# Inputs laid out in order of need on one DMA queue, three warm-up products instead of four, and the head's steps put in another order

## What is computed

```python
x = x + L0: x @ (sum_g y[b,g] * weight[g] * mask).T + bias          # a weight per batch
x = x + L1: x @ W_base.T + b_base + 2 * sum_e w[b,e] * (x @ A[e].T) @ B[e].T   # rank 16 each
x = x + L2: sum over the top 2 of 8 experts of w * mlp_e(x) + mlp_shared(x)    # gelu(x@G)*(x@U)@D, 512 wide
x = x + L3: mlp of the argmax expert, silu(up)*gate, 256 wide, with biases
```

## Time and profile before

| | us |
|---|---|
| median of 3 runs | 142.79 (141.63 to 143.33) |
| the profiled execution | 141.64, span 139.8 |
| PE busy | 134.5 (96%) |
| DVE busy | 100.2 (72%) |
| ACT busy | 97.9 (70%) |
| POOL busy | 73.9 (53%) |
| chain that ended last | PE 93% of the span |

### The profile page before, as it was taken

The page is one execution under the profiler, slowest core; times in us unless marked ns, Lnnn a source line. Parts: engine busy times, 40 slices in busy tenths (PEclk is TensorE's granted clock), DMA queues, the critical chain, the costliest instruction groups (busy, mean ns, idle before and its releaser), DMA issues.

```text
span 139.8 us, 3283 instructions
## 1 busy us (share of the span) xinstructions
PE 134.5 (96%) x932; PEld 124.2 (89%) x932; DVE 100.2 (72%) x192; ACT 97.9 (70%) x201; POOL 73.9 (53%) x87
## 2 busy tenths in 40 slices
PE   6989999989999999999999999999999999999991
PEld 5768888768888899999999999999999999999991
DVE  0587898695775957758768577676767766878983
ACT  3394697867985487777877777757657569887770
POOL 0229349772995028358496574962542625325370
PEclk9999999999999999999999999999999999999999
DMA  4899999998000895656756567555576465773215
GB/s 126 261 408 412 403 400 401 400 388 326 9 0 0 334 369 210 259 217 273 291 209 254 210 246 300 224 231 233 217 301 259 199 264 217 279 298 152 77 42 187
DMA packets 11346, 34.56 MB, mean 247 GB/s; under 512 B 1088, under 2 KB 2240, under 8 KB 11328
## 3 DMA queue, kind: packets, MB, share of 16 engines
q1 hardware_dynamic: 11040, 33.82, 61.8%
q10 hardware_dynamic: 288, 0.52, 1.1%
HBM read 12.32 MB, written 1.05 MB: 96 GB/s over the span
## 4 chain that ended last, share of the span: by engine, by line
PE 93%; DVE 2%; ACT 1%; issue 1%; ACTq 0%; DVEq 0%
PE acc L284 31%; PE up L284 31%; PE gate L284 30%; DVE x_res L935 1%; ACT h_hi L589 1%; DVE h_lo L970 0%; ACT out_part L630 0%; ACT h_act L651 0%; DVE slabs L822 0%; ACTq L213 0%; DVE slabs L782 0%; ACTq L607 0%; DVE shift_pick L783 0%; ACT dn_hi L607 0%; ACT h_act L583 0%
## 5 line engine op out<-in xcount | busy, mean ns | idle before, releaser
L721 POOL TENSOR_TENSOR dn_lo<-slabs,dn_hi 128x256 fp32r<-128x256 f32 x40 | 29.6, 739 | 42.7 <-ACT dn_hi L607 42.6
L583 ACT ACTIVATE h_act<-gate 128x512 f32<-128x512 f32 x48 | 28.8, 599 | 27.7 <-PE gate L284 26.3
L875 DVE SCALAR_TENSOR_TENSOR up<-h_act,w_route,up 128x512 f32<-128x512 f32 x32 | 24.2, 756 | 20.5 <-PE up L284 20.5
L865 DVE TENSOR_TENSOR h_lo<-up,h_hi 128x512 fp32r<-128x512 f32 x55 | 37.6, 684 | 0.4 <-ACT h_hi L589 0.4
L284 PE MATMUL gate<-x_hi,w_gu 128*128 128x256 f32 x160 | 35.5, 282 | 0.2 <-ACT h_act L651 0.2
L284 PE MATMUL up<-x_hi,w_gu 128*128 128x256 f32 x160 | 35.4, 281 | 0.0
L589 ACT ACTIVATE h_hi<-up 128x512 fp32r<-128x512 f32 x55 | 32.8, 596 | 0.0
L284 PEld LDWEIGHTS gate<-x_hi,w_gu 128*128 128x128 f32 x160 | 27.6, 189 | 0.7 <-issue 0.4
L284 PEld LDWEIGHTS up<-x_hi,w_gu 128*128 128x128 f32 x160 | 27.7, 189 | 0.0
L284 PE MATMUL up<-x_lo,w_gu 128*128 128x256 f32 x80 | 22.6, 283 | 0.0
L284 PE MATMUL gate<-x_lo,w_gu 128*128 128x256 f32 x80 | 22.6, 283 | 0.0
(11 more groups left out here) (115 smaller groups left out, 213.9 us busy)
## 6 DMA issues: line engine op xcount, KB each, us to landing
w_gu<-slabs SPq DMA_DIRECT2D x40, 512.0 KB, 3.0
slabs<-slabs_moe SPq DMA_DIRECT2D x8, 768.0 KB, 14.8
slabs<-slabs_l SPq DMA_DIRECT2D x4, 768.0 KB, 8.2
outT<-x_res SPq DMA_DIRECT2D x8, 128.0 KB, 2.0
sh_raw<-slabs_shared SPq DMA_DIRECT2D x2, 384.0 KB, 7.5
x_res<-xT SPq DMA_DIRECT2D x1, 768.0 KB, 8.1
slabs<-w_l SPq DMA_DIRECT2D x2, 256.0 KB, 4.1
slabs<-lin ACTq DMA_DIRECT2D x1, 384.0 KB, 4.9
```

The source lines that it names most:

```text
L583: nc.scalar.activation(h_act[:, u % 2, :], gate_ps[u % 2][:], ACT.Gelu_apprx_tanh).then_inc(act_done, 1)
L721: nc.gpsimd.tensor_tensor(dn_lo[:, q % W_SLOTS, :], slab_cols(at, DOWN_AT, 256), dn_hi[:, q % W_SLOTS, :].bitcast(F32), ALU.subtract).then ...
L865: V.tensor_tensor(h_lo[:, u % H_SLOTS, :], h_of(u), h_hi[:, u % H_SLOTS, :].bitcast(F32), ALU.subtract).then_inc(h_lo_done, 1)
L875: ins = V.scalar_tensor_tensor(h_of(u), h_act[:, k, :], weight, h_of(u), ALU.mult, ALU.mult)
```

## The change

Five tensors take the place of four. first_in holds cond and the first half of w_l0 (762 columns), second_in the other half, lora_bT and mask (768 columns), third_in lora_a, w_baseT, ident and lora_aT (512 columns). x is given as two tensors, x_first and x_rest, and the shared weights as two halves, each contiguous in memory. All are issued by SP, in that order; ACT issues none. Warm-up products go from four to three. ACT scales lora_bT for all eight batches, in the order 0 1, 2 3 4 5, 6 7, and DVE for none. ACT rounds the first half of the shared weights ahead of exp_pick and the gelu table. POOL makes the remainder of that half ahead of the slab table. keep_x2 of pairs 2 and 3 stands ahead of product and lo_h.

```diff
-WARM_UP = 4
+WARM_UP = 3
...
-            sp.dma_start(w_l0_sb[:, 0:4, :], w_l0[:, 0:4, :]).then_inc(d_w_l0, DMA)
-            sp.dma_start(w_l0_sb[:, 4:8, :], w_l0[:, 4:8, :]).then_inc(d_w_l0b, DMA)
-            sp.dma_start(x_res[:, 0:PAIR], xT[:, 0:PAIR]).then_inc(d_x, DMA)
-            sp.dma_start(sh_raw[:, 0:SLAB], slabs_shared[:, 0:SLAB]).then_inc(d_shared[0], DMA)
-            sp.dma_start(x_res[:, PAIR:], xT[:, PAIR:]).then_inc(d_x_rest, DMA)
-            sp.dma_start(sh_raw[:, SLAB:], slabs_shared[:, SLAB:]).then_inc(d_shared[1], DMA)
+            sp.dma_start(cond_all[:, :], first_in).then_inc(d_first, DMA)
+            sp.dma_start(second_sb[:, :, :], second_in).then_inc(d_second, DMA)
+            sp.dma_start(third_sb[:, :, :], third_in).then_inc(d_third, DMA)
+            sp.dma_start(x_res[:, 0:PAIR], x_first).then_inc(d_x, DMA)
+            sp.dma_start(sh_raw[:, 0:SLAB], slabs_shared[0]).then_inc(d_shared[0], DMA)
+            sp.dma_start(sh_raw[:, SLAB:], slabs_shared[1]).then_inc(d_shared[1], DMA)
+            sp.dma_start(x_res[:, PAIR:], x_rest).then_inc(d_x_rest, DMA)
...
-            pe.wait_ge(d_lin, DMA)
-            for out, first_b, n, ready in ((gate_ps[0][:, 0:S], 0, 2, bw_first), (up_ps[1][:, 0:S], 6, 2, bw_last),
-                                           (gate_ps[1][:], 2, 4, bw_middle)):
-                pe.wait_ge(ready, 1)
...
+            pe.wait_ge(d_third, DMA)
...
+            pe.wait_ge(bw_ready, 1)
+            lora(gate_ps[0][:, 0:S], 0, 2)
+            mm(acc_ps[:, 512:512 + B], lora_aT, bias_l0.to_broadcast([P, B]), True, True).then_inc(a_bias_sum, 1)
+            pe.wait_ge(bw_ready, 2)
+            lora(gate_ps[1][:], 2, 4)
...
             matrix(0)
+            pe.wait_ge(bw_ready, 3)
+            lora(up_ps[1][:, 0:S], 6, 2)
...
-            act.dma_start(cond_all[:, :], cond).then_inc(d_cond, DMA)
-            act.dma_start(lin_sb[:, :, :], lin).then_inc(d_lin, DMA)
...
-            act.wait_ge(d_lin, DMA)
+            act.wait_ge(d_second, DMA)
             act.wait_ge(scaled_ready, 1)
-            for group, ready in (((6, 7), bw_last), ((2, 3, 4, 5), bw_middle)):
+            for group in ((0, 1), (2, 3, 4, 5), (6, 7)):
...
+            round_shared(0)
             act.wait_ge(top2_ready, 1)
             act.wait_ge(zeros_ready, 2)
             nc.scalar.activation(exp_pick[:], shift_pick[:], ACT.Exp).then_inc(second_ready, 1)
             nc.scalar.activation(table_first[:, 0:1], cond_sb[:, 0, 0:1], ACT.Gelu_apprx_tanh)
...
-            round_shared(0)
...
             nc.gpsimd.tensor_tensor(key[:], hit[:, 1], rows(rank_e, B), ALU.mult).then_inc(key_ready, 1)
+            lo_shared(0)
...
-            lo_shared(0)
             lo_shared(1)
...
-            V.tensor_tensor(lora_bw[:, 0:2], rows(lora_bT, 2),
-                            cond_scaled[:, 0:2].unsqueeze(2).to_broadcast([P, 2, P]),
-                            ALU.mult).then_inc(bw_first, 1)
...
+            mask_w0(0)
             dve.wait_ge(shift_ready, 1)
...
+            mask_w0(1)
             dve.wait_ge(base_ready, 1)
...
-            add_base(1, 6, 2, up_ps[1][:, 0:S])
+            add_base(1, 2, 4, gate_ps[1][:])
+            dve.wait_ge(r1_ready, 1)
+            combine(0)
+            add_base(2, 6, 2, up_ps[1][:, 0:S])
             dve.wait_ge(key_ready, 1)
             V.tensor_reduce(first[:, 1], key[:], AX_X, ALU.max).then_inc(first_ready, 1)
-            dve.wait_ge(r1_ready, 1)
-            combine(0)
             dve.wait_ge(c_sum, 1)
             V.tensor_scalar(c_b[:], acc_ps[:, 0:B], bias_l1, None, ALU.add).then_inc(acc_read, ACC_BIAS)
-            add_base(2, 2, 4, gate_ps[1][:])
...
                 if u - 1 in X2_AFTER_UNIT:
                     split_x2(X2_AFTER_UNIT[u - 1])
+                    if u > 1:
+                        keep_x2(X2_AFTER_UNIT[u - 1])
                 product(u)
                 lo_h(u - 1)
-                if u - 1 in X2_AFTER_UNIT:
-                    keep_x2(X2_AFTER_UNIT[u - 1])
+                if u == 1:
+                    keep_x2(X2_AFTER_UNIT[0])
```

More of the change, by code:

```diff
@@ L65, with build @@
 C_VECS = C_RANK + E
-C_COLS = C_VECS + 2 + 5 * E
-def build(nc, xT, cond, w_l0, lin, slabs_moe, slabs_l3, slabs_shared, outT):
+C_W = C_VECS + 2 + 5 * E
+C_COLS = C_W + 4 * P
+def build(nc, x_first, first_in, second_in, third_in, x_rest, slabs_moe, slabs_l3, slabs_shared, outT):
     with ExitStack() as ctx:
@@ L173, in build @@
         scaled_ready, bias_prod_ready = sem("scaled_ready"), sem("bias_prod_ready")
[L174 to L175 removed]
+        bw_ready, base_ready = sem("bw_ready"), sem("base_ready")
         pool_step = sem("pool_step")
@@ L573, in _ @@
             round_shared(0)
+            act.wait_ge(top2_ready, 1)
+            act.wait_ge(zeros_ready, 2)
+            nc.scalar.activation(exp_pick[:], shift_pick[:], ACT.Exp).then_inc(second_ready, 1)
+            nc.scalar.activation(table_first[:, 0:1], cond_sb[:, 0, 0:1], ACT.Gelu_apprx_tanh)
             act.wait_ge(x2_first_sum, 1)
@@ L973, in _, with cond_layout @@
                 finish(t)
-def cond_layout(cond, vecs):
+def cond_layout(cond, vecs, w_l0):
     p = np.arange(P)
@@ L985, in cond_layout @@
     c[:, C_RANK:C_VECS] = E - np.arange(E)
-    c[:, C_VECS:] = vecs
+    c[:, C_VECS:C_W] = vecs
+    c[:, C_W:] = w_l0.reshape(P, 4 * P)
     return c
```

63 lines of the change are left out of this document (28 added, 35 removed).

## The result

| | median of the runs | ratio to before (95% interval) | profiled execution |
|---|---|---|---|
| before | 141.94 us (22 runs) | | 141.64, span 139.8 |
| changed | 141.38 us (22 runs) | 0.9928 (0.9904 to 0.9952) | 141.52, span 139.6 |

The ratio makes 1.0 us of 141.94; forecast were 1.4 us and 141.4. The two profiled executions differ by only 0.1 us, though, and that is the question of this study: the work ends 1.3 us earlier, and in the profiled execution the end of the program takes 1.1 us of it back.

The account below looks back on a forecast made before the run. The prediction took a chain of waits on TensorE nearly everywhere as the bound, with gains only in the head and the stream's stops. 0.6 + 0.05 + 0.75 = 1.4 us, 142.79 - 1.4 = 141.4 us; range 140.2 to 143.0.

Parts of the forecast that it names:

- Landings: Transfers at the start: first_in lands at 4.4 us, second_in at 5.4, third_in at 6.05 or a little before, slab at 7.7.
- Rival A: Start of the kernel: first_in lands at 4.1 and the rest with it, 0.3 to 0.5 us more gain, 140.9; chance 0.2.
- Rate of x_first: Transfers from 6 to 7 us: a contiguous x_first is read at the full rate, not 146 GB/s; slab at 7.7, not 8.8.
- rival B: Landings gain nothing: second_in not before 6.05 us (142.0), or slab at 8.8 (total gain 1.15 us); chance 0.23.
- The head, 0.6: Before TensorE's stream: second_in at 5.4 starts ACT's scalings earlier, matrix(0) comes at 8.47 against 9.13; gain passed on 0.6 us.
- is not on the path by itself: TensorE's start: one warm-up product fewer lets it begin at 4.4 instead of 4.9 us, 0.25 us to it, no gain alone.
- ACT's order: ACT before the stream: slab rounding, exp_pick, table load and table_first end at 10.4 us, just before x_hi is wanted at 10.6.
- The stream, 0.75: Shared stage: keep_x2 moved earlier removes TensorE's waits before x2(3), 0.15 us, and unit 4's first down product, 0.6 us.
- Rival C: Shared stage: the earlier keep_x2 makes product(6) late; the stream gains 0.2 us, total 0.85, 141.9; chance 0.1.
- rival D: TensorE's clock stays low past matrix(0) with three warm-ups: 1.3 to 2.3 us slower, 144.1 to 145.1; chance 0.12.
- The sum: Whole kernel: gains of 0.6, 0.05 and 0.75 make 1.4 us, taken from a median of 142.79.
- a shift of the stream stays a shift: After the shared stage: the chain stays on TensorE to the last units, weights land in time, so gains of 1.4 us last.

Follow-up runs that it names:

- two queues for the outputs: The changed kernel with two of its eight output transfers (fifth and seventh) issued by ACT, the rest by SP; 139.91 us, ratio 0.985.
- slices kernel: The changed kernel with x given as one tensor and read as two slices with a row pitch of 8 KB; 142.86 us, ratio 1.003.
- keep_x2 alone: The kernel before with only keep_x2 of pairs 2 and 3 moved ahead of product and lo_h; 141.36 us, ratio 0.994.
- three, two small, again: Second measurement of the changed kernel with two products of eight columns added behind its three warm-up products; 141.61 us, ratio 0.994.
- two queues in the head: The changed kernel with second_in and third_in issued by ACT instead of SP; 141.54 us, ratio 0.993.
- two variants: The kernel before with only keep_x2 of pairs 2 and 3 moved earlier, 141.36 us (0.994), and with three warm-up products instead of four, 142.64 us (1.002).
- two small products: The changed kernel with two products of eight columns added behind its three warm-up products; 140.65 us, ratio 0.989.
- one warm-up product and eight small ones: The changed kernel with one warm-up product and eight products of 8 columns in place of three warm-up products; 143.09 us, ratio 1.003.

## Why the prediction was right, and where a term was off

The forecast of the median and the two causes, landings in order of need and keep_x2 out of the way, were right. The path through the head was not, and two terms met their sizes because errors cancelled.

- **Landings.** Right in order and nearly in time. First was mis-sized, 3.7 against 4.4: one queue alone brings 381 KB in 3.0 us, with a second queue beside it 4.0.
- **Rival A**, first at 4.1 or earlier and a faster head with it, was half true: first came even sooner, but the head was no faster than forecast, as PE's products on first were still at the lower clock. With an early rise as well (two queues for the outputs, rise at 4.13) the stream started at 11.20, 0.56 us earlier than in the changed kernel, a little over rival A's price of 0.3 to 0.5. The table load then held x_hi to 10.64, as its "against" had it.
- **Rate of x_first.** I took it that contiguous reading ends the dip; the slices kernel shows it, with more at stake (1.4 us by the two ratios) than rival B had given it (0.25 us: 1.15 instead of 1.4). B had the slab at 8.8; it came at 10.2.
- **The head, 0.6.** Measured 12.36 - 11.76 = 0.60, but by another path. The prediction let everything depend on second through ACT's scalings, and said of PE's earlier start that it "is not on the path by itself". Second landed at 5.22 and six scalings were over at 7.1; by the forecast's own 0.23 us the 512-column product would have started at 7.34. It started at 7.60, behind PE's masked products at the lower clock. A landing 0.2 us early and products 0.3 us late cancelled; that matrix(0) came at 8.5 is luck. The eleven profiles with the changed head bear the path out: put in order of the end of PE's first eight masked products (5.12 to 7.51 us), they are in order of x2 as well (9.10 to 13.03, the two at 5.84 within 0.02), while the landing of second does not order them (4.73 with x2 at 9.10, 4.63 with 10.52, 5.83 with 10.41).
- **ACT's order.** x_hi was just covered: table_first ends at 10.41, x_hi starts at 10.62. The new orders on ACT, DVE and POOL were not taken back one by one, so what each is worth in the 0.6 is not shown. The Trainium skill's page "ScalarE: Activation LUTs", section "What ACT_TABLE_LOAD costs", would have put 2.66 us where the row has 1.28 with 0.02 us on either side; the measurement decides. By the page's figure x_hi would have started near 11.8, an estimate.
- **The stream, 0.75.** From the stream's start to DVE's last addition the changed kernel won 1.33 - 0.60 = 0.73, and keep_x2 alone 0.77 - 0.12 = 0.65. The closeness is luck again. Up to unit 4 the step won 0.99 and 0.92, and in the seven profiles with keep_x2 moved in which PE does not wait for w_gu it is 1.04 to 1.07 to the end: the term was too small by 0.3, and both kernels lost about as much at the w_gu of 50.9 and 51.45 us. Why that transfer is late in some executions stays open; a 16 KB packet of q8 is in flight shortly before it lands (48.7 to 49.7 us in the changed kernel), which no run tests. Rival C, a late product(6), shows nowhere.
- **The clock, rival D.** It did not come as priced in the changed kernel, but the mechanism is real, and its bound was too late: D was to decide only from a rise later than about 7.4 us, and with the rise at 6.86 (three, two small, again) x2 came at 10.52, so that the head had won nothing. Among the kernels with three warm-ups and the changed head (small products or not) the rise lay at 4.13, 4.47, 4.57, 5.64, 6.31, 6.5, 6.67 and 6.86 us, and x2 at 9.10 to 10.52; with two queues in the head, where no rise is recorded, the products were at the lower level to 8.5 us and x2 came at 11.32. The kernel before and its two variants had x2 at 10.40 to 10.52 with rises from 4.74 to 6.29, since there the wait for lin covers the slower products. The change thus made the head depend on the clock; the small products add to it where they are, since they hold PE to 4.6 instead of 3.9 us. The Trainium skill's page "TensorE: Matmul & The Clock Gate", section "What's actually happening", says that the moment of the rise varies from run to run of one kernel; the two profiles of the changed kernel, 6.67 and 5.64, agree.
- **The sum.** 1.4 forecast, 1.33 at DVE's last addition, 1.0 (0.7 to 1.4) in the median. That 141.38 met the forecast 141.4 so closely is luck: it was worked out from a median of three runs, 142.79, and that of 22 is 141.94, from which 1.4 would have made 140.5. The statement that failed is "a shift of the stream stays a shift": 0.3 us were lost at the w_gu of 50.9 us, and between the last addition and the last landing another 1.1 us in the profiled execution. I had read the end of the trace before as fixed cost, without asking what its issues were close to.

**What is shown of the tail, and what is not.** In seven of the fourteen profiles one output issue takes 1.05 to 1.84 us. In all seven a 16 KB packet of q8 is in flight during it, the issue ahead of it on SP lies at most 0.7 us back, and it ends 0.34 to 0.38 us after the packet does, which is about the length of an undisturbed issue. Not only SP is late: the output issued just ahead of the long one lands 2.6 to 3.6 us after its issue, where all others but the long ones take 1.9 to 2.3. An issue that overlaps only the packet's first 0.2 us or less can still be short (0.43 us at 133.87 with two small products). In the seven others the packet is over, or meets a single issue that follows none within 1.2 us and takes 0.33 us; the kernel before has such a one at 134.25 us, within its packet from 133.94 to 135.36. So by all appearance the issue waits for the packet's end; that this is the cause rests on these 14 profiles, not on an experiment that moved the packet alone. Why the packet lies where it does stays open: it lay 0.9 us apart in two executions of one program, 2.9 us apart with one warm-up product fewer, and hardly apart with two small ones more. The Trainium skill's page "Runtime: NRT & Kernel Launch", section "Instruction fetch mechanics", says that instructions are fetched in 16 KiB blocks over a DMA queue of the engine's own and that the cost is mostly hidden. The size agrees with the packets of q8. That it is mostly hidden agrees only in part: where the packet met closely spaced output issues, the tail was 0.7 to 1.4 us longer. The medians agree only loosely, since the clock's rise moves them by as much.

## What to carry to other kernels

Put what the first engine needs alone on a queue and make it contiguous: a second queue cost the first landing 1.0 us, and slices with a pitch of 8 KB cost the slab behind them 2.3. Follow a gain to the last landing: with the last outputs issued one behind the other within half a microsecond, half of the profiles here lost 0.7 to 1.4 us beside a 16 KB packet. Spreading them over two queues gave the lowest median, but the block itself was never met with two queues, so that it escapes it is not shown. When a wait is shortened, ask what it had covered: here it was the spread of the clock's rise. And when a time comes out as forecast, look at what released each step before calling the path right.

## What the runs showed that I had not expected

- An issue of SP may take 1.8 us instead of 0.33 while a 16 KB instruction packet of another queue is in flight.
- The clock's rise, with three warm-up products (in three kernels with two small ones behind), came between 4.1 and 6.9 us in eight profiles, and at 11.3 us after one warm-up product and eight small ones.
- The transfer of the third w_gu (512 KB) took 4.9 us from issue to landing instead of 2.9 to 3.0 in five profiles, and PE lost some 0.3 us to it in the middle of the stream.
- 256 KB read with a row pitch of 8 KB went at 125 GB/s, where contiguous reads go at 393 to 409 in the same place.
- Medians of one program on two occasions, each beside the kernel before, gave ratios of 0.9928 and 0.9883; a difference of 0.5% between two kernels needs both on one chip, and more than six runs.
